# Moving the layer norm of two row tiles from between the attention blocks into the next block

## The reference

```python
def _layernorm(x, axis=-1, eps=1e-5):
    m = jnp.mean(x, axis=axis, keepdims=True)
    v = jnp.var(x, axis=axis, keepdims=True)
    return (x - m) / jnp.sqrt(v + eps)

def _L0_attn_ref(x, Wq, bq, Wk, bk, Wv, bv, Wo, bo):
    ...
    Q = (x @ Wq + bq) * scale
    K = (x @ Wk + bk) * scale
    V = x @ Wv + bv
    Qr = jnp.transpose(Q.reshape(B * H, dk, L), (0, 2, 1))
    Kr = K.reshape(B * H, dk, L)
    w = jnp.matmul(Qr, Kr)
    w = jax.nn.softmax(w.astype(jnp.float32), axis=-1).astype(w.dtype)
    Vr = jnp.transpose(V.reshape(B * H, dv, L), (0, 2, 1))
    a = jnp.matmul(w, Vr).reshape(B, L, D)
    return a @ Wo + bo

def _L0_ffn_ref(x, W1, b1, W2, b2):
    ...
    def _quantize(W):
        gamma = jnp.mean(jnp.abs(W))
        return jnp.clip(jnp.round(W / (gamma + EPS)), -1.0, 1.0)
    h = jax.nn.relu(jnp.einsum('bsd,fd->bsf', x, _quantize(W1)) + b1)
    return jnp.einsum('bsf,df->bsd', h, _quantize(W2)) + b2

x = _layernorm(x + _L0_attn_ref(x, ...))
x = _layernorm(x + _L0_ffn_ref(x, ...))
```

## Time and profile before

| | |
|---|---|
| two runs | 3466.5 and 3518.8 us, median 3492.7 us |
| the profiled execution | 3464.5 us, its span 3463.0 us (the 8 cores: 3449.9 to 3463.0) |
| ACT, Exp L520 | 2048 of 1105 ns, busy 1889.1 us |
| PE busy | 2749.5 us, 79% of the span |
| DVE busy | 914.7 us, 26% of the span |
| POOL busy | 153.3 us, 4% of the span |
| chain that ended last, by engine | ACT 46%, PE 22%, issue 11%, DMA 11%, DVE 6% |

### The profile page before, as it was taken

The page is one execution under the profiler, slowest core; times in us unless marked ns, Lnnn a source line. Parts: engine busy times, 40 slices in busy tenths (PEclk is TensorE's granted clock), DMA queues, the critical chain, the costliest instruction groups (busy, mean ns, idle before and its releaser), DMA issues.

```text
span 3463.0 us, 40735 instructions; the slowest of 8 cores (3449.9 to 3463.0 us)
## 1 busy us (share of the span) xinstructions
PE 2749.5 (79%) x12064; PEld 893.6 (26%) x12064; DVE 914.7 (26%) x1371; ACT 1948.2 (56%) x2307; POOL 153.3 (4%) x282
## 2 busy tenths in 40 slices
PE   1899999717899998227999996147999995799998
PEld 0322222202222222102222222012222221344443
DVE  0212222232122223322223333321321112343343
ACT  0199999600899997002999995004999993000000
POOL 3000000000000000000000000000000000000000
PEclk9899999858999999658999998568999997899999
DMA  8401111145011111234121112252110005721111
GB/s 110 67 30 44 38 37 43 53 100 73 18 41 44 44 32 55 85 77 62 42 62 60 56 55 65 81 82 38 55 49 8 6 8 112 126 84 43 37 49 43
DMA packets 171946, 191.59 MB, mean 55 GB/s; under 512 B 113248, under 2 KB 129632, under 8 KB 171616
## 3 DMA queue, kind: packets, MB, share of 16 engines
q1 hardware_dynamic: 141536, 158.37, 18.6%
q0 software_dynamic: 30208, 30.62, 5.1%
HBM read 125.93 MB, written 37.88 MB: 47 GB/s over the span
## 4 chain that ended last, share of the span: by engine, by line
ACT 46%; PE 22%; issue 11%; DMA 11%; DVE 6%; SPq 2%; ACTq 1%; POOL 1%; DVEq 0%; POOLq 0%
ACT PT L520 45%; PE ps_sb L773 6%; PE ps_pv L720 6%; PE ps_pv L434 4%; DMA Wch<-W 3%; DMA x_bf<-x 3%; SPq L579 1%; PE ps_tr L475 1%; ACTq L29 1%; DMA x_tc<-x 1%; PE ps_pv L533 1%; PE ps_sb L507 1%; DMA Kd<-Qtm 1%; PE ps_pv L430 1%; DMA wq<-qout 1%
## 5 line engine op out<-in xcount | busy, mean ns | idle before, releaser
L520 ACT ACTIVATE PT<-ps_sb 128x1024 bf16<-128x1024 f32 x2048 | 1889.1, 1105 | 86.4 <-PE ps_sb L512 84.6
L533 PE MATMUL ps_pv<-PT,VsT 128*65 128x512 bf16 x2048 | 828.9, 405 | 20.8 <-ACT PT L520 20.8
L507 PE MATMUL ps_sb<-Qd,Kd 64*128 64x512 bf16 x2048 | 758.6, 375 | 78.0 <-ACT PT L520 70.1
L512 PE MATMUL ps_sb<-Qd,Kd 64*128 64x512 bf16 x2048 | 785.2, 388 | 0.0
L538 PE MATMUL ps_pv<-PT,VsT 128*65 128x512 bf16 x2048 | 778.7, 380 | 0.0
L546 DVE RECIPROCAL rec_sb<-ps_pv 1x512 f32<-1x512 f32 x64 | 214.5, 3352 | 874.1 <-PE ps_pv L538 874.1
L507 PEld LDWEIGHTS ps_sb<-Qd,Kd 64*128 64x128 bf16 x2048 | 185.4, 93 | 928.2 <-issue 928.2
L533 PEld LDWEIGHTS ps_pv<-PT,VsT 128*65 128x65 bf16 x2048 | 221.2, 108 | 514.2 <-issue 514.2
L653 ACT ACTIVATE uln<-vareps 128x1 f32<-128x1 f32 x16 | 3.2, 203 | 503.3 <-DVE vareps L649 503.3
L720 PE MATMUL ps_pv<-x1T,WqT 128*128 128x512 bf16 x1024 | 230.8, 389 | 27.5 <-DMA x1T<-x1bfscr 14.5
L390 PE MATMUL ps_tr<-eye,x_bf 128*128 128x128 bf16 x128 | 32.2, 266 | 270.5 <-DMA x_bf<-x 239.3
(11 more groups left out here) (90 smaller groups left out, 1236.7 us busy)
## 6 DMA issues: line engine op xcount, KB each, us to landing
Wch<-W SPq DMA_DIRECT2D x128, 512.0 KB, 3.8
Qd<-Qtm SPq DMA_DIRECT2D x32, 256.0 KB, 6.2
Kd<-Qtm SPq DMA_DIRECT2D x32, 256.0 KB, 6.1
rec_bc<-recscr POOLq DMA_DIRECT2D x64, 128.0 KB, 2.8
x_tc<-x SPq DMA_DIRECT2D x16, 512.0 KB, 3.8
wqt<-qout SPq DMA_DIRECT2D x64, 128.0 KB, 1.7
wq<-qout SPq DMA_DIRECT2D x64, 128.0 KB, 1.9
x1f<-x1scr SPq DMA_DIRECT2D x16, 512.0 KB, 3.9
```

The lines of the kernel that those rows point to most:

```text
L507: sch.add(t, lambda e, cc=cc, qt=qt, hh=hh: e.matmul(ps_sb[:, hh:hh + 512], Kd[0:64, cc * 128:cc * 128 + 128], Qd[0:64, qt * 512:qt * 512 ...
L512: ts = sch.add(t, lambda e, cc=cc, qt=qt, hh=hh: e.matmul(ps_sb[:, hh + 512:hh + 1024], Kd[64:128, (cc + 1) * 128:(cc + 1) * 128 + 128], Q ...
L520: ex = sch.add(sc, lambda e, gg=gg: e.activation(PT[:, (gg % 4) * 1024:(gg % 4) * 1024 + 1024], ps_sb[:, (gg % 2) * 1024:(gg % 2) * 1024 + ...
L533: sch.add(t, lambda e, pg=pg, qtg=qtg: e.matmul(ps_pv[qtg % 2][0:65, :], VsT[:, (2 * pg) * 65:(2 * pg) * 65 + 65], PT[:, (pg % 4) * 1024:( ...
```

## The change

`emit_ln1` is split in two. The first part, `emit_ln1_a`, is DVE's sum, mean, subtraction, squares and variance; the variance now goes to a column of a new small tile `lnva` that each `tc` has for itself. The second, `emit_ln1_b`, is ACT's Ln and Exp, DVE's multiply and the write to `x1scr`. For tc=0 and tc=1 both are emitted at once, as before. For tc=2 and tc=3 of every block both go to `deferred_ln`. In block `b` from 1 on these parts of block `b-1` are emitted ahead of tile 2 (first part of tc=2), tile 4 (second part of tc=2, first of tc=3) and tile 6 (second part of tc=3), and there also POOL's waits and the copy to `x1bfscr`. Block 3's stay where they were.

```diff
     rstd = alloc("rstd", [128, 1], F32)
     warm = alloc("warm", [1, 256], BF16)
     b1c = alloc("b1c", [128, 32], F32)
+    lnva = alloc("lnva", [128, 4], F32)
 
     A0 = off[0]
 
@@ -488,8 +489,24 @@
             wp[("vstS", b)] = (sSC, sch.v(sSC))
 
             PVLAG = 2
+            dstate = {}
             for qt in range(QTB):
                 qtg = b * QTB + qt
+                if deferred_ln and b > 0:
+                    if qt == 2:
+                        dstate["a2"] = deferred_ln[0][0]()
+                    elif qt == 4:
+                        deferred_ln[0][1](dstate["a2"])
+                        dstate["a3"] = deferred_ln[1][0]()
+                    elif qt == 6:
+                        deferred_ln[1][1](dstate["a3"])
+                        deferred_ln.clear()
+                        bb = b - 1
+                        sch.w(g, sX1W[0], wp[("x1w", bb, 2)][1])
+                        sch.w(g, sX1W[1], wp[("x1w", bb, 3)][1])
+                        sch.add(g, lambda e, bb=bb: e.dma_start(
+                            AP(x1bfh, bb * 524288, [[1024, 512], [1, 1024]]),
+                            AP(x1scrh, bb * 524288, [[1024, 512], [1, 1024]])), sCB[bb], 16)
                 for gg in range(NGQ + PVLAG):
                     gi = gidx_of(b, qt, gg)
                     if gg < NGQ:
@@ -630,7 +647,7 @@
                     wp[("s1evac", b, tc)] = (sVE, ev)
                 if tc == 3:
                     mark(("outproj", b), sTT)
-                def emit_ln1(b=b, tc=tc):
+                def emit_ln1_a(b=b, tc=tc):
                     sl = (tc % 2) * 1024
                     if b > 0 or tc >= 2:
                         bb, tt = (b, tc - 2) if tc >= 2 else (b - 1, tc + 2)
@@ -646,11 +663,16 @@
                         x1[:, sl:sl + 1024], s1[:, sl:sl + 1024], 1.0,
                         s1[:, sl:sl + 1024], ALU.mult, ALU.mult,
                         accum_out=varsum[:, :]), sVE)
-                    lv = sch.add(v, lambda e: e.tensor_scalar(
-                        vareps[:, :], varsum[:, :], 1.0 / 1024.0, LN_EPS,
+                    lv = sch.add(v, lambda e, tc=tc: e.tensor_scalar(
+                        lnva[:, tc:tc + 1], varsum[:, :], 1.0 / 1024.0, LN_EPS,
                         ALU.mult, ALU.add), sVE)
+                    return lv
+
+                def emit_ln1_b(lv, b=b, tc=tc):
+                    sl = (tc % 2) * 1024
                     sch.w(sc, sVE, lv)
-                    sch.add_sync(sc, lambda e: e.activation(uln[:, :], vareps[:, :], AF.Ln), sSC)
+                    sch.add_sync(sc, lambda e, tc=tc: e.activation(
+                        uln[:, :], lnva[:, tc:tc + 1], AF.Ln), sSC)
                     sr = sch.add(sc, lambda e: e.activation(
                         rstd[:, :], uln[:, :], AF.Exp, scale=-0.5), sSC)
                     sch.w(v, sSC, sr)
@@ -665,18 +687,12 @@
                         AP(x1scrh, (b * 512 + tc * 128) * 1024, [[1024, 128], [1, 1024]]),
                         x1[:, sl:sl + 1024]), xsem, 16)
                     wp[("x1w", b, tc)] = (xsem, 32 if gq else xw)
-                if b < NB - 1 or tc < 2:
-                    emit_ln1()
+                if tc < 2:
+                    emit_ln1_b(emit_ln1_a())
                 else:
-                    deferred_ln.append(emit_ln1)
+                    deferred_ln.append((emit_ln1_a, emit_ln1_b))
                 emit_qstep()
                 emit_qstep()
-            if b < NB - 1:
-                sch.w(g, sX1W[0], wp[("x1w", b, 2)][1])
-                sch.w(g, sX1W[1], wp[("x1w", b, 3)][1])
-                sch.add(g, lambda e, b=b: e.dma_start(
-                    AP(x1bfh, b * 524288, [[1024, 512], [1, 1024]]),
-                    AP(x1scrh, b * 524288, [[1024, 512], [1, 1024]])), sCB[b], 16)
 
         while qstate["i"] < len(qsteps):
             emit_qstep()
@@ -736,8 +752,9 @@
             if b + 1 < NB:
                 emit_x1t(b + 1)
             if b == 0:
-                for f in deferred_ln:
-                    f()
+                for fa, fb in deferred_ln:
+                    fb(fa())
+                deferred_ln.clear()
                 bb = NB - 1
                 sch.w(g, sX1W[0], wp[("x1w", bb, 2)][1])
                 sch.w(g, sX1W[1], wp[("x1w", bb, 3)][1])
```

## The result

The changed kernel takes 3386.39 us (median of 11 runs, lowest 3384.13); the kernel before, run beside it, 3468.61 (median of 10, lowest 3466.52). The ratio is 0.9768, 95% interval 0.9731 to 0.9805: the gain is clear of noise, but that it is over 2% is not quite shown, since the interval reaches to 0.9805. The forecast was 3392, range 3375 to 3430. In some executions of every kernel here the cores of one die, or of both, show a lower granted clock and take some per cent longer, so that the lowest runs are compared where a median contains such executions (run 7), and of run 5 only cores 0 to 3 are read.

The account below looks back on a forecast made before the run. ACT was taken to bound attention, single loads and DVE's order the stretches between blocks. Gains 80.9 less costs 4.0, 3.0 and 1.2 gave 72.7; 3464.5-72.7 = 3391.8 us, range 3375 to 3430.

Parts of the forecast that it names:

- What bounds it: ACT bounds attention; between blocks nothing is busy and single loads end the chain, so shortening there shortens the kernel one for one.
- Gains of 80.9: Layer norm of tc=2 and 3 leaves the three stretches between attention blocks: 26.5, 27.0 and 27.4 us gained.
- `x_tc` beside `Wch`, 4.0: Both loads fly together at tc=2 and 3 of the last two stretches between attention blocks: 1.0 us at four places.
- Early `x_bf`, 3.0: The first two x_bf loads, now at the start of each between-block stretch, disturb its first loads: 1.0 us each.
- ACT pairs, 1.2: Six Ln and Exp pairs at starts of tiles 4 and 6 hide in ACT's idle time; 0.2 us each.
- DVE, 0: Moved layer norm work nearly fits DVE's idle time in attention; a late reciprocal costs nothing, from 0 to 1 us.
- Rival 1: Between blocks, x_tc waits out the whole Wch load and x_bf costs 2.9 us instead of 1.0: 3410 us; chance 15%.
- Rival 2: In attention, each of six moved layer norm chains costs its 6.05 us again, 36.3 in all: 3428 us; chance 10%.
- Rival 3: At tiles 4 and 6 ACT waits at the Ln for DVE, 25 us six times: 3542 us, slower; chance 3%.
- Rival 4: ACT switches tables between Ln and Exp after all, 15.4 us: 3407 us; chance 2%.

Follow-up runs that it names:

- run 7: Changed kernel with quantisation and gamma steps taken out of the output projection and emitted only behind attention tiles, three per tile while gamma, then two; 3254.59 us.
- run 5: Changed kernel plus 54 further ACT pairs of Ln and Exp on own data, one at a tile's start; 3444.95 us.
- run 2: Changed kernel, but SP waits for the evacuation of tc=2 and tc=3 of blocks 0 to 2 before the next Wch load; 3416.17 us.
- run 3: Kernel before, with only POOL's two waits and copy to x1bfscr moved ahead of tile 6 of the next block, layer norms unmoved; 3449.42 us.
- runs 9 and 10: 9: changed kernel with x_tc loads issued further ahead, 3367.21 us; 10: that, plus quantisation and gamma steps only behind tiles 0 to 14, 3173.76 us.
- run 4: Changed kernel, but POOL issues the first two x_bf loads of blocks 1 to 3 only after tc=2 of the block before is evacuated; 3392.41 us.
- run 1: Changed kernel with both layer norm parts together again, tc=2 whole ahead of tile 2, tc=3 whole ahead of tile 4; 3559.86 us.

## Why the prediction was right, step by step

**What bounds it.** Right. The transitions were on the path one for one: 78.1 us gone there, 82 in the medians of all runs (3468.61-3386.39) and 3464.5 to 3386.4 by the profiled execution's own time. By the mean span of the eight cores runs 2, 3 and 7 moved the whole by 24.0, 13.2 and 152.9, where their transitions moved by 22.3, 14.4 and 152.4; runs 9 and 10 gained 4 and 7 less than there, since the feed-forward part took some back.

**Gains of 80.9.** Right in size and place. The three parts, from the runs: the load that is hidden now about 22 (run 2); POOL's copy away from the last load, net of the earlier `x_bf`, 14 (run 3); the rest, 41, is what DVE's layer norm and SP's write had cost. Run 2 shows what that was. SP issues `Wch` there right behind the evacuation, which ends at 1449.56:

```profile
1449.70 0.34 SPq L265 DMA_DIRECT2D Wch<-W  x1
```

That is 0.14 us behind it instead of 6.05, 5.9 at each of six places, 35.5. Besides, the load itself is there sooner when it no longer follows the write of `x1`: on the means of eight cores by 0.5 to 0.8 us at tc=2 (beside the kernel before) and by 0.5 to 1.0 at tc=3 (beside run 3), 4.4 in all. The two make 39.9. In B the pieces came as worked out: step to evacuation 1455.20-1436.98 = 18.2 (18.1 forecast), the two steps to the copy 1472.77-1459.04 = 13.7 (14.4 forecast with the gap). A also had its gamma load late by a little, as said for tc=3:

```profile
728.09 1.22 DVE L254 TENSOR_REDUCE gtmp<-Wch 128x1 f32<-128x1024 f32 x1 [0.55 <-DMA Wch<-W]
...
735.47 0.69 DVE L636 SCALAR_TENSOR_TENSOR s<-ps_sb,x_tc 128x512 f32<-128x512 f32 x1
...
739.52 1.22 DVE L254 TENSOR_REDUCE gtmp<-Wch 128x1 f32<-128x1024 f32 x1 [0.83 <-DMA Wch<-W]
```

**`x_tc` beside `Wch`, 4.0.** Too dear. DVE waits 4.67 and 4.50 us for `x_tc` in B on core 3, where core 7 waited 3.94 at tc=3 before. On the means of eight cores the four waits of B and C are 4.42, 4.46, 4.56 and 4.84 instead of 4.20, 4.19, 4.35 and 4.27: 0.3 a place, 1.3 in all. The row of 4.9 us on which the 1.0 rested is a median over three loads of transition A with other neighbours.

**Early `x_bf`, 3.0.** Right in kind, a little too dear. Up to the first evacuation the transitions are 1.1, 0.1 and 0.8 longer than before, 2.0 together, and 2.8 in run 3, which moves the same loads. What they had cost at tc=3, in the time of before, is in the gains already, which take the steps there as undisturbed; run 4, which puts them back there without the copy, loses 4.2 at that place.

**ACT pairs, 1.2.** Zero. In the changed kernel ACT at the start of tile 4 of block 1:

```profile
972.54 0.30 ACT L674 ACTIVATE uln<-lnva 128x1 f32<-128x1 f32 x1
972.93 0.20 ACT L676 ACTIVATE rstd<-uln 128x1 f32<-128x1 f32 x1
973.98 29.44 ACT L537 ACTIVATE PT<-ps_sb 128x1024 bf16<-128x1024 f32 x32 [0.84 <-PE ps_sb L529]
1004.63 5.76 ACT L537 ACTIVATE PT<-ps_sb 128x1024 bf16<-128x1024 f32 x6 [1.21 <-PE ps_sb L529]
```

The wait of 1.21 us is there with the pair or without it; with it, 0.84 of idle time is left behind 0.6 of work and gaps. Run 5 confirms it for 54 more pairs.

**DVE, 0.** Right, and the overflow that was foreseen did occur, at tile 4 of block 3:

```profile
2465.13 0.75 DVE L679 TENSOR_SCALAR x<-s,rstd 128x1024 f32<-128x1024 f32 x1 [0.18 <-DVE qout L348]
...
2469.76 3.35 DVE L563 RECIPROCAL rec_sb<-ps_pv 1x512 f32<-1x512 f32 x1
```

The reciprocal starts with no idle time before it, so DVE was late; the next ones are on time and the block is no longer than before (460.91).

Net, the transitions came 4.2 us better than 80.9-4.0-3.0 = 73.9, and attention 1.2 better: 5.4 of the 5.6 by which 3392 missed. Of the 4.2 the cheaper `x_tc` is 2.7 and the cheaper `x_bf` 1.0; the rest, 0.5, is below what two executions differ by. The three costs were all set too high, so the total came near not by errors that cancel, but because the gains, by far the largest term, were right: 78.1 with the 1.3 and 2.0 added back is 81.4, against 80.9.

**The rivals.** Rival 1 (queueing loads): the mean waits for `x_tc` are 4.4 to 4.8 us at the four places, and a single one of 32 on the eight cores is over 5.1 (5.88, in C), not well over 5 as it stated; out. Rival 2 (attention gives it back): no block is longer by more than 0.2 us; out. Rival 3 (ACT stalls at the Ln) is real in run 1 and absent with the two-tile lead. Rival 4: the groups by line still have

```profile
L239 ACT ACT_TABLE_LOAD x1 | 1.3, 1283 | 6.3 <-DVE acc L235 6.3
```

one load for the whole program, and run 5 with 54 more pairs has one too and is no slower on cores 0 to 3. The Trainium skill, "ScalarE: Activation LUTs", section "What ACT_TABLE_LOAD costs", asks that price only for a change of set; with Ln and Exp in one set, as its list has it, the trace agrees.

## What to carry to other kernels

Where an in-order queue issues both loads and writes that wait for a result, look at what stands behind each wait: here such a write exposed a 4 us load at six places, 22 us, and in each transition two `x_tc` loads still stood so. Work may go from a stretch that waits on round trips into one that another engine bounds, but its part on that bounding engine must be queued late enough that its input is surely there, and at a place where the engine has a hole anyway. Don't read the value of a wait from its total: 446 us of waiting vanished with 82 us of time.
